# Edge sums without ring copies: GpSimd waits slot by slot, and VectorE makes all seventeen one-hots of a body

## The reference

```python
def _rgcn_layer(X, W, root, bias, gamma, beta, src, dst, etype, inv_deg):
    h = jnp.einsum('ni,rio->rno', X, W)
    msg = h[etype, src] * inv_deg[:, None]
    agg = jax.ops.segment_sum(msg, dst, num_segments=X.shape[0])
    out = agg + X @ root + bias
    mu = jnp.mean(out, axis=-1, keepdims=True)
    var = jnp.mean(jnp.square(out - mu), axis=-1, keepdims=True)
    out = (out - mu) * jax.lax.rsqrt(var + EPS) * gamma + beta
    out = jax.nn.elu(out)
    return out + X
```

## Time and profile before

| | |
|---|---|
| median of 3 runs | 7984.36 us (7972.84 to 7988.71) |
| profiled execution | 7983.88 us, its span 7982.1 us |
| TensorE (PE) | 5806.8 us busy, 73% |
| VectorE (DVE) | 4250.2 us busy, 53% |
| ScalarE (ACT) | 2839.0 us busy, 36% |
| GpSimd (POOL) | 4226.4 us busy, 53%; 4003.6 of it the 4165 gathers (L537) |
| one-hots | VectorE 620.0 us (L546, 1764), ScalarE 625.0 and 645.9 us (L515, L527) |
| ring copies | 490 of L502, 95.0 us |

### The profile page before, as it was taken

The page is one execution under the profiler, slowest core; times in us unless marked ns, Lnnn a source line. Parts: engine busy times, 40 slices in busy tenths (PEclk is TensorE's granted clock), DMA queues, the critical chain, the costliest instruction groups (busy, mean ns, idle before and its releaser), DMA issues. The chain is left out here.

```text
span 7982.1 us, 89847 instructions
## 1 busy us (share of the span) xinstructions
PE 5806.8 (73%) x17886; PEld 3446.9 (43%) x17886; DVE 4250.2 (53%) x14583; ACT 2839.0 (36%) x7998; POOL 4226.4 (53%) x4288
## 2 busy tenths in 40 slices
PE   0488888878777777777778888786597777763398
PEld 0244444444444444444433333454344444442265
DVE  7216665657776666666656666323434666642412
ACT  0134444434444455555533333221123443421122
POOL 0017777767777666666667777200004777743211
PEclk9799999888998888899966555797798787876699
DMA  1444444444444444444443333100244333320000
GB/s 57 140 137 132 132 131 131 131 135 143 144 143 142 139 129 128 127 129 128 129 133 105 105 105 105 49 0 0 75 136 125 106 106 106 106 72 1 13 14 18
DMA packets 479425, 815.31 MB, mean 102 GB/s; under 512 B 88660, under 2 KB 343208, under 8 KB 478716
## 3 DMA queue, kind: packets, MB, share of 16 engines
q0 software_dynamic: 200480, 548.02, 24.0%
q1 hardware_dynamic: 278488, 262.51, 10.0%
HBM read 614.04 MB, written 196.16 MB: 102 GB/s over the span
## 5 line engine op out<-in xcount | busy, mean ns | idle before, releaser
L537 POOL DMA_INDIRECT gnn_msg<-tables,gnn_row_ring x4165 | 4003.6, 961 | 1900.2 <-issue 1513.9
L585 PE MATMUL bank<-gnn_msg,gnn_hot 128*128 128x256 f32 x8330 | 3117.4, 488 | 861.9 <-DVE sums L566 559.5
L566 DVE TENSOR_TENSOR sums<-sums,bank 128x256 f32 x4165 | 1746.7, 419 | 1821.1 <-PE bank L585 1145.2
L585 PEld LDWEIGHTS bank<-gnn_msg,gnn_hot 128*128 128x128 f32 x8330 | 1709.2, 232 | 2262.4 <-issue 1256.8
L134 POOL TENSOR_TENSOR ve<-mv,eps 128x7 f32<-128x7 f32 x35 | 7.2, 205 | 1349.7 <-DVE mv L128 1201.9
L527 ACT ACTIVATE gnn_hot<-gnn_away,gnn_meta_ring 128x128 f32<-128x128 f32 x1568 | 645.9, 482 | 47.3 <-ACT gnn_meta_ring L518 0.8
L696 PE MATMUL bank<-gnn_w,residual 128*128 128x512 f32 x1176 | 646.1, 634 | 0.0
L515 ACT ACTIVATE gnn_away<-iota,gnn_meta_ring 128x128 f32<-128x128 f32 x1960 | 625.0, 390 | 25.3 <-DMA residual<-in_L_mix_b_dram 14.0
L546 DVE TENSOR_SCALAR gnn_hot<-iota,gnn_meta_ring 128x128 f32<-128x128 f32 x1764 | 620.0, 352 | 0.5 <-ACT gnn_meta_ring L503 0.5
L502 ACT COPY gnn_row_ring<-row 128x9 int32<-128x9 int32 x490 | 95.0, 194 | 798.2 <-PE bank L585 786.2
L670 ACT ACTIVATE gnn_own<-gnn_own 128x256 f32<-128x256 f32 x196 | 81.6, 416 | 800.8 <-DVE gnn_own L650 800.8
(11 more groups left out here) (389 smaller groups left out, 6524.4 us busy)
## 6 DMA issues: line engine op xcount, KB each, us to landing
tables<-residual SPq DMA_DIRECT2D x294, 256.0 KB, 2.8
gnn_msg<-tables,gnn_row_ring POOLq DMA_INDIRECT x4165, 2.7
tables<-sums SPq DMA_DIRECT2D x98, 512.0 KB, 2.9
tables<-gnn_msg SPq DMA_DIRECT2D x98, 256.0 KB, 2.1
residual<-first_norm_columns SPq DMA_DIRECT2D x98, 128.0 KB, 4.0
first_norm<-state SPq DMA_DIRECT2D x1, 6272.0 KB, 22.2
first_rows<-residual SPq DMA_DIRECT2D x1, 6272.0 KB, 39.1
residual<-first_norm SPq DMA_DIRECT2D x49, 128.0 KB, 3.8
```

The source lines that it names most:

```text
L537: self.nc.gpsimd.indirect_dma_start(out=self.msg[:, s0 + u, :], out_offset=None, in_=table, in_offset=bass.IndirectOffsetOnAxis(ap=self.ro ...
L566: self.nc.vector.tensor_tensor(at, at, self.sums(s, phase), ALU.add).then_inc(self.added, 1)
L585: self.nc.tensor.matmul(self.sums(s, phase), self.hot[:, s, :], self.msg[:, s, :], start=True, stop=True).then_inc(self.summed, 1)
```

## The change

The ring is gone, and so are its copies. The gather and the one-hots read the tables of all steps directly. GpSimd waits, for each slot, until the step that held it in the body before is multiplied (17 waits for two). ScalarE makes no one-hots. VectorE makes the one-hot of step s of the next body right behind its add of step s, so 17 a body. The register load of the next body's tiles moves from the start of that body to the place behind step 11 of the body before, into a second set of registers; the two sets take turns. TensorE waits for the one-hot and the bank ahead of the message. `gnn1`'s GpSimd starts on the row numbers of its layer alone.

```diff
-DVE_HOTS = (5, 4)
-ACT_HOTS = 4
-NEXT_HOTS = (((), (), (0,), (), (1,), (), (2,), (), (3,)),
-             ((), (), (0,), (1,), (), (2,), (3,), (4,)))
+TILES_AT = 11
...
-def body_tiles(eng, c, i):
-    regs = c.regs[str(eng.engine)]
-    eng.reg_load(regs, c.body_row[0:1, ds(i * (SLOTS + 1), SLOTS + 1)])
+def body_tiles(eng, c, n):
+    regs = c.regs[n % 2]
+    eng.reg_load(regs, c.body_row[0:1, ds(n % NT * (SLOTS + 1), SLOTS + 1)])
...
+    def gpsimd(self, pool, n, table):
+        for s in range(SLOTS):
+            if n:
+                pool.wait_ge(self.summed, (n - 1) * SLOTS + s + 1)
+            at = n % NT * SLOTS + s
+            self.nc.gpsimd.indirect_dma_start(
+                out=self.msg[:, s, :], out_offset=None, in_=table,
+                in_offset=bass.IndirectOffsetOnAxis(ap=self.rows[:, at:at + 1], axis=0)).then_inc(self.landed[s], 16)
+
+    def one_hot(self, n, s):
+        at, c = n % NT * SLOTS + s, self.c
+        to, local, weight = self.hot[:, s, :], c.local[:, at:at + 1], c.weight[:, at:at + 1]
...
+    def begin_vector(self, dve, n):
+        for s in range(SLOTS):
+            self.one_hot(n, s)
+        self.tiles = body_tiles(dve, self.c, n)
+
+    def vector(self, dve, n, after, last=False):
+        tiles = self.tiles
+        for s in range(SLOTS):
+            dve.wait_ge(self.summed, n * SLOTS + s + 1)
+            if n or s:
+                dve.wait_ge(self.added, n * SLOTS + s)
+            at = self.c.agg[:, ds(tiles[s] * D, D)]
+            self.nc.vector.tensor_tensor(at, at, self.sums(n, s), ALU.add).then_inc(self.added, 1)
+            if not last:
+                self.one_hot(n + 1, s)
+            after(s)
+            if s == TILES_AT and not last:
+                self.tiles = body_tiles(dve, self.c, n + 1)
...
-                        edges.ring(act, i + 1, n + 1, 0)
-                        edges.scalar_hots(act, n, 1)
                         post.turned(act, n, t)
-                        edges.scalar_hots(act, n + 1, 0)
                         post.way_out(act, n, 0)
-                        edges.ring(act, i + 1, n + 1, 1)
                         post.way_out(act, n, 1)
```

More of the change, by code:

```diff
@@ L492, in sums @@
[L492 to L516, removed]
+        self.hot_ready, self.summed, self.added = (c.sem(n) for n in ("hot_made", "steps_summed", "steps_added"))
@@ new lines, in __init__, with use, sums @@
+        self.tiles = None
+    def use(self, msg, hot, rows, weighted):
+        self.msg, self.hot, self.rows, self.weighted = msg, hot, rows, weighted
+    def sums(self, n, s):
+        return self.c.bank[4 + (n * SLOTS + s) % SUM_SLOTS][:, 0:D]
+    def gpsimd(self, pool, n, table):
[6 more added lines that the diff above has]
+                in_offset=bass.IndirectOffsetOnAxis(ap=self.rows[:, at:at + 1], axis=0)).then_inc(self.landed[s], 16)
@@ L522, in scalar_hots @@
[L522 to L548, removed]
+            ins = self.nc.vector.tensor_scalar(to, c.iota[:], local, None, ALU.is_equal)
         ins.then_inc(self.hot_ready, 1)
@@ L551, in begin_vector @@
     def begin_vector(self, dve, n):
[L553 to L573, removed]
@@ L586, in tensor @@
+    def tensor(self, pe, n, after):
+        for s in range(SLOTS):
+            pe.wait_ge(self.hot_ready, n * SLOTS + s + 1)
+            if n * SLOTS + s >= SUM_SLOTS:
+                pe.wait_ge(self.added, n * SLOTS + s - SUM_SLOTS + 1)
+            pe.wait_ge(self.landed[s], n * 16 + 16)
+            self.nc.tensor.matmul(self.sums(n, s), self.hot[:, s, :], self.msg[:, s, :], start=True, stop=True).then_inc(self.summed, 1)
             after(s)
-def each_body(eng, first, last, body):
-    for i in range(first, last):
-        body(i, i)
@@ L1266, in _ @@
                     work.begin_tensor(pe)
-                    edges.tensor(pe, l * NT, l * NT, work.tensor(pe, 0, True, False))
+                    edges.tensor(pe, l * NT, work.tensor(pe, 0, True, False))
                     pe.wait_ge(s_w, (l + 2) * 64)
[L1270 to L1274, removed]
+                    for i in range(1, NT):
+                        edges.tensor(pe, i + l * NT, both(post.tensor(pe, i + l * NT), work.tensor(pe, i, True, True)))
                     drain(both(post.tensor(pe, (l + 1) * NT), work.tensor(pe, NT, False, True)))
@@ L1278, in _ @@
                     pe.sem_inc(s_tabs, 1)
-                def last_body(i, phase):
-                    edges.tensor(pe, i + LASTL * NT, phase + LASTL * NT, nothing)
-                each_body(pe, 0, NT, last_body)
+                for i in range(NT):
+                    edges.tensor(pe, i + LASTL * NT, nothing)
             @block.scalar
@@ L1330, in _ @@
                     act.wait_ge(kept, NG * 32 + 32)
-                act.wait_ge(s_root, NT)
-                for h in range(2):
-                    edges.ring(act, 0, 0, h)
-                edges.scalar_hots(act, 0, 0)
                 act.wait_ge(s_keep, 32)
@@ L1337, in _ @@
                     work.begin_scalar(act)
-                    edges.scalar_hots(act, l * NT, 1)
                     work.scalar(act, 0, True, False)
-                    edges.ring(act, 1, l * NT + 1, 0)
-                    edges.scalar_hots(act, l * NT + 1, 0)
-                    edges.ring(act, 1, l * NT + 1, 1)
-                    def body(i, phase):
+                    for i in range(1, NT):
                         n = i + l * NT
@@ L1390, in _ @@
                     gate(pool, c)
-                    each_body(pool, 0, NT, lambda i, phase: edges.gpsimd(pool, i + l * NT, c.tabs[l % 2]))
+                    for i in range(NT):
+                        edges.gpsimd(pool, i + l * NT, c.tabs[l % 2])
             @block.vector
             def _(dve):
-                dve.sem_inc(edges.added, SLOTS)
                 dve.wait_ge(s_vec, 48)
@@ L1413, in _ @@
                     gate(dve, c)
-                    edges.vector(dve, body_tiles(dve, c, 0), l * NT, l * NT, work.vector(dve, 0, True, False))
+                    edges.vector(dve, l * NT, work.vector(dve, 0, True, False))
                     dve.wait_ge(s_vec, l * 48 + 96)
-                    def body(i, phase):
+                    for i in range(1, NT):
                         n = i + l * NT
-                        tiles = body_tiles(dve, c, i)
-                        edges.vector(dve, tiles, n, phase + l * NT,
-                                     both(post.vector(dve, n, tiles[SLOTS], work.cols), work.vector(dve, i, True, True)))
-                    each_body(dve, 1, NT, body)
+                        edges.vector(dve, n, both(post.vector(dve, n, edges.tiles[SLOTS], work.cols), work.vector(dve, i, True, True)))
                     t = ranked_tile(dve, c, NT - 1)
@@ L2012, in _ @@
                 keys.begin_tensor(pe)
-                edges.tensor(pe, n0, n0, keys.tensor(pe, 0, True, False))
-                each_body(pe, 1, NT, lambda i, phase: edges.tensor(pe, i + n0, phase + n0, keys.tensor(pe, i, True, True)))
+                for i in range(NT):
+                    edges.tensor(pe, i + n0, keys.tensor(pe, i, True, i > 0))
                 drain(keys.tensor(pe, NT, False, True))
@@ L2545, in program @@
                    (("pe", nc.tensor), ("act", nc.scalar), ("dve", nc.vector), ("pool", nc.gpsimd), ("sp", nc.sync))}
-        c.regs = {str(e.engine): [e.alloc_register(f"tile{u}") for u in range(SLOTS + 1)] for e in (nc.vector,)}
+        c.regs = [[nc.vector.alloc_register(f"tile{n}_{u}") for u in range(SLOTS + 1)] for n in range(2)]
         c.rank_reg = {str(e.engine): e.alloc_register("ranked") for e in (nc.vector, nc.scalar, nc.sync)}
```

106 lines of the change are left out of this document (20 added, 86 removed).

## The result

The changed kernel takes 8024.36 us (median of 4 runs, 8018.63 to 8031.09) against 7980.11 for the kernel before (4 runs): 1.0055 times the time, 95% interval 1.0038 to 1.0073. It is slower by 44 us where 106 us were expected to go. The profiled execution spans 8021.8 us.

A forecast was written before the change was run, and what follows sets the result against it. GpSimd's gathers were taken as the floor, with the loop of VectorE, ScalarE and TensorE limiting layers 1 and 2. Layers 0 to 3 give 25 - 6 + 84 + 3 = 106 us: 7983.88 - 106 = 7878, range 7800 to 7985.

The forecast's parts named there:

- One-hots: VectorE: eight more a body at up to 0.26 us each, 2.08 us a body in layer 1, 100 us over 48 bodies.
- the wait for the exponential: VectorE in layer 2, before L653: two one-hots fill 0.52 of its 1.65 us a body, 25 us.
- ScalarE's chain and the waits at adds 13 to 15: Chain from L661 to add 13 shortens from 5.56 to 4.0 us; 223, 94 and 159 us of waits go in layers 0 to 2.
- the forecast's share for short loads: In half of the bodies the load's idle time, 1.5 us, counts as TensorE's: 36 us a layer that move and stay.
- GpSimd's floor and the gathers: GpSimd needs at least 1042.6 us a layer for 833 gathers; their median stays 0.947 us.
- the prediction's third rival: One-hots hold back GpSimd's gathers: eight more add 2.7 us a body, 8482 us in all; chance 0.02.
- The failed step: TensorE during the load behind step 11: its stall delays no other engine, as products and evictions have a body's time.
- A term put at nothing: The register load holds VectorE's queue for 1.56 to 5.16 us, median 1.96, wherever it stands.
- the pauses between layers: GpSimd between layers: pauses end on the stored tables, 86.3 us in three times, and stay.
- the waits for TensorE stay, slower: Rival at adds 12 to 15: one-hots lengthen VectorE's body, the moved load covers nothing, 8221 us if nothing is recovered; chance 0.11.

## Why the prediction was wrong

**One-hots: right.** 1.27 + 0.49 + 0.26 = 2.02 us a body in layer 1 for 2.08, 1.60 in layer 2 for 1.56 (there the wait for the exponential falls from 76.1 us, 48 times, to 51.3, 47 times, 0.5 us a time).

**ScalarE's chain and the waits at adds 13 to 15: right.** 94 / 48 = 1.96 us a body were to go in layer 1, and 1.97 went; 159 / 48 = 3.31 in layer 2, and 3.31 went. In both, 0.26 of it is time that the one-hot of step 13 now fills: the adds themselves lie 1.71 and 3.05 us closer. That it agrees to the hundredth is luck, since the forecast's share for short loads was an estimate. The reason given was half of it: the load behind step 11 was not needed for this. With the load at the body's end the waits are gone too, by ScalarE's freedom alone, and with the old one-hots the load alone removes most of them (from add 12 to add 15, 3.32 and 3.61 us for 4.95 and 5.83).

**GpSimd's floor and the gathers: right.** Median 946 ns with seventeen one-hots a body for 947 with nine. The Trainium skill, "SBUF — State Buffer", section "Who interferes with whom", says that `tensor_scalar` can enter a mode that takes the ports shared with GpSimd, if its operands meet conditions; the prediction's third rival took that for every one-hot. These medians show none of it for 128x128 one-hots in float32, whatever mode they ran in.

**The failed step** is the sentence on the moved load: "TensorE is four banks ahead and stalls in the load, but with nothing queued behind it that another engine needs before VectorE is back". Something was queued there: L632 of step 15, which needs VectorE's L600, three adds behind the load, and matmuls 16 and 0 behind it, which VectorE needs. The sentence took the products as work that has a body's time to be done, not as places in TensorE's queue. TensorE's hook of step 15 and VectorE's of step 14 stand in the code with one semaphore between them, so this could have been read there. The price is 2.28 and 2.05 us a body in layers 1 and 2, 48 x 4.33 = 208 us. Where the load stands behind step 14, or L600 ahead of the load, adds 16 and 0 take 1.5 and 0.64 us, and the kernel is 199 and 137 us faster.

**A term put at nothing**: the sum takes the load to cost the same at either place. It costs 0.65 and 0.55 us a body less behind step 11, 48 x 1.20 = 58 us. With the stall that makes 208 - 58 = 150 us, and the forecast of 7878 is missed by 146.

**A smaller one**: the pauses between layers were taken as unchanged. Where VectorE's loop sets the pace they grew, 27.2 to 39.4 and 30.3 to 39.5 us, 21 in all. This is no further loss: VectorE's bodies account for the time from first gather to first gather by themselves, and the pauses are the part of it that GpSimd's windows don't show. In the kernel before with slot waits alone the pauses grow as well (36.1 and 39.4), and with the load behind step 14 they are 22.0, 23.5 and 38.9. GpSimd may be a whole body ahead with slot waits, half with rings, so its last gather of a layer comes earlier than VectorE's last add; that reason is argued, the pauses are measured.

The rival "the waits for TensorE stay, slower" had the sign but not the place: adds 13 to 15 are free of waits, add 12 has the idle time of the load alone, 16 and 0 have them, and its cause (a chain that starts late) is not what happened.

**Left open**: what part of the 3.76 us in a body with a long load is the lowered clock. The products take 2.08 + 1.92 us there against 1.12 + 1.02 in the short one, so about 1.9 us by these two bodies, an estimate; no run changes the clock alone. Why TensorE keeps enough lead with the load behind step 8 to stall, and how it loses it step by step, was not followed.

## What to carry to other kernels

When a blocking operation is moved along an in-order engine, look not only at what it now covers but at the first semaphore behind it that another engine waits for, and at what stands behind that wait in the other engine's queue. A stall that an engine's slack takes up costs nothing (layer 0 here, and layer 1 with nine one-hots) until another edit spends that slack: two edits that gain 128 us alone (the load behind step 11) and 70 alone (the rest, with the load behind step 16) lost 44 together, and only the runs of one without the other showed it. Where half of a group of loads takes 2.5 us longer than the other, look at the addresses before the schedule.

## What the runs showed of the hardware

VectorE's load of 18 registers takes 1.57 us or 4.06 us and more, in turn by body, with rows 72 bytes apart; with rows 80 or 128 bytes apart all are short (medians 1.70 and 1.57 us). A row that begins at a multiple of 16 bytes would explain all three; no other pitch was tried. A load runs beside the last operations ahead of it, and its place changes its price: 3.52 us a body at the end in the kernel before, 2.64 behind step 14 (7.59 - 4.95), of which 0.28 is a wait that it covers there. In the two bodies shown, 4.71 us of idle time of TensorE were followed by a granted clock of 0.50, 1.76 us were not.
